# Reordering the matrix engine's work in the opening slot of sequences two to seven

## What is computed

```python
q, k, v = split(x @ Wqkv + bqkv)                       # heads of 32 columns
q_prime = exp(q @ omega - 0.5 * |q|^2); k_prime = exp(k @ omega - 0.5 * |k|^2)
k_sum = sum over rows of k_prime;  k_v = k_prime.T @ v # one per sequence and head
out = (q_prime @ k_v) / (q_prime @ k_sum + 1e-6)
x = layernorm(x + out @ Wout + bout)
x = layernorm(x + x @ weight.T + pooled(x) @ disha)
```

## Time and profile before

| | |
|---|---|
| median of three runs | 2395.49 us (2395.23 to 2403.92) |
| the profiled execution | 2395.51 us, of which its span is 2393.7 us |
| granted TensorE clock, mean | 0.998 of 2.4 GHz |
| PE busy | 2343.8 us, 98% of the span |
| DVE busy | 1956.4 us, 82% |
| ACT busy | 1268.2 us, 53% |
| POOL busy | 286.7 us, 12% |
| SyncE's transfers, issue to landing (median) | 2.1 to 5.0 us |

### The profile page before, as it was taken

The page is one execution under the profiler, slowest core; times in us unless marked ns, Lnnn a source line. Parts: engine busy times, 40 slices in busy tenths (PEclk is TensorE's granted clock), DMA queues, the critical chain, the costliest instruction groups (busy, mean ns, idle before and its releaser), DMA issues.

```text
span 2393.7 us, 55214 instructions
## 1 busy us (share of the span) xinstructions
PE 2343.8 (98%) x21224; PEld 1325.2 (55%) x21224; DVE 1956.4 (82%) x3751; ACT 1268.2 (53%) x2281; POOL 286.7 (12%) x390
## 2 busy tenths in 40 slices
PE   8999999999999999999999999999999999999997
PEld 4545555555555555555555555555555555555554
DVE  6778887888888888887888878888778888788776
ACT  4555555555555555555555555555555555555443
POOL 0001111011111011111011110111110111100221
PEclk9999999999999999999999999999999999999999
DMA  6322332323323323323323233233233232232231
GB/s 209 90 74 71 108 80 82 94 82 94 101 71 99 94 68 108 87 76 96 89 85 104 73 92 95 76 100 98 66 106 90 72 108 76 86 77 59 73 102 50
DMA packets 160277, 213.11 MB, mean 89 GB/s; under 512 B 19376, under 2 KB 119824, under 8 KB 156048
## 3 DMA queue, kind: packets, MB, share of 16 engines
q1 hardware_dynamic: 159440, 208.53, 31.3%
q10 hardware_dynamic: 576, 1.05, 0.1%
HBM read 73.19 MB, written 33.55 MB: 45 GB/s over the span
## 4 chain that ended last, share of the span: by engine, by line
PE 87%; DVE 7%; issue 3%; ACT 2%; SPq 0%; DMA 0%; DVEq 0%; POOL 0%; POOLq 0%; ACTq 0%
PE bank_y L459 24%; PE bank_a L459 24%; PE bank_x L459 12%; PE bank_kf L524 4%; PE bank_qf L578 4%; PE kv_ps L550 3%; PE bank_nm L609 3%; PE bank_x L626 3%; PE bank_nm L626 1%; DVE q_feat_lo L843 1%; PE bank_nm L614 1%; PE kv_ps L556 1%; PE bank_x L486 1%; PE bank_a L486 1%; PE kv_ps L459 1%
## 5 line engine op out<-in xcount | busy, mean ns | idle before, releaser
L706 ACT ACTIVATE q_feat<-bank_qf 128x512 f32<-128x512 f32 x512 | 305.8, 597 | 183.9 <-PE bank_qf L578 183.7
L836 DVE TENSOR_TENSOR k_feat_lo<-k_feat 128x512 bf16<-128x512 f32 x512 | 367.2, 722 | 43.3 <-ACT k_feat L696 43.3
L696 ACT ACTIVATE k_feat<-bank_kf 128x512 f32<-128x512 f32 x512 | 306.0, 598 | 169.7 <-PE bank_kf L524 137.5
L843 DVE TENSOR_TENSOR q_feat_lo<-q_feat 128x1024 bf16<-128x1024 f32 x256 | 313.3, 1224 | 12.3 <-ACT q_feat L706 10.7
L987 POOL TENSOR_TENSOR rstd<-mean_var,minus_half 128x1 f32<-128x1 f32 x128 | 70.3, 549 | 1648.1 <-DVE mean_var L919 1648.1
L976 POOL TENSOR_TENSOR rows<-rows,bias_out 128x512 f32<-128x512 f32 x128 | 168.2, 1325 | 442.1 <-DMA rows<-x 440.2
L524 PE MATMUL bank_kf<-omega_s,stack_k 98*128 98x128 f16 x1920 | 185.8, 219 | 3.1 <-ACT k_feat L696 2.7
L550 PE MATMUL kv_ps<-v_both,k_feat 128*128 128x65 f16 (+1 forms) x2048 | 181.3, 190 | 5.9 <-DVE k_feat_lo L836 5.3
L578 PE MATMUL bank_qf<-stack_q,omega_s 98*128 98x256 f16 x960 | 183.7, 272 | 1.2 <-ACT q_feat L706 1.2
L556 PE MATMUL kv_ps<-v_both,k_feat_lo 128*128 128x33 f16 x2048 | 182.6, 179 | 0.0
L524 PEld LDWEIGHTS bank_kf<-omega_s,stack_k 98*128 98x128 f16 x1920 | 136.1, 97 | 77.6 <-issue 23.5
(11 more groups left out here) (206 smaller groups left out, 5147.7 us busy)
## 6 DMA issues: line engine op xcount, KB each, us to landing
rows<-x SPq DMA_DIRECT2D x128, 256.0 KB, 2.9
out<-rows SPq DMA_DIRECT2D x128, 256.0 KB, 2.1
xt_f<-xt SPq DMA_DIRECT2D x31, 1024.0 KB, 5.0
stack_k<-t_hi_k SPq DMA_DIRECT2D x240, 128.0 KB, 2.4
stack_q<-t_hi_q SPq DMA_DIRECT2D x240, 128.0 KB, 2.4
stack_k<-t_lo_k SPq DMA_DIRECT2D x120, 128.0 KB, 2.4
stack_q<-t_lo_q SPq DMA_DIRECT2D x120, 128.0 KB, 2.4
stack_q<-t_hi_k SPq DMA_DIRECT2D x16, 128.0 KB, 2.5
```

The source lines that it names most:

```text
L696: nc.scalar.activation(k_feat[:, i % 2, :], bank_kf[:, :], ACT.Exp, scale=1.0 / WS).then_inc(S["k_exp"], 1)
L706: nc.scalar.activation(q_feat[:, 2 * pair:2 * pair + 2, :], bank_qf[:, :].rearrange("p (e n) -> p e n", e=2), ACT.Exp, scale=1.0 / WS).the ...
L836: v.tensor_tensor(k_feat_lo[:, u, :], k_feat[:, u, :], k_feat_hi[:, u, :], ALU.subtract).then_inc(S["kfl"], 1)
L843: v.tensor_tensor(q_feat_lo[:, at, :], q_feat[:, at, :], q_feat_hi[:, at, :], ALU.subtract).then_inc(S["qfl"], 2)
```

## The change

A ninth order, `ORDER_NEXT`, is used in the opening slots of b = 2 to 7, six slots in all. It differs from `ORDER` in one line and a half, and no piece is added or removed. TensorE does the second half of FF3' before NM1 and not after it. KF0 moves ahead of the second half of VP1. AT0 and NM2 move behind that half. KF1 and KV0 move ahead of WO0's first half, and NM3 and QF8 between its halves. The orders of ScalarE, VectorE and GpSimd are derived from the same string and change with it. SyncE's order is the same as before.

```diff
@@ -68,6 +68,14 @@
+ORDER_NEXT = """
...
 (the lines ahead of these are those of ORDER; of ORDER:)
-QP2 FF3'. NM1 FF3' VP1. AT0 NM2 Z3' KF0 VP1 QF8 NM3 WO0. KF1 QF9 WO0 KV0 KF2 VP2. AT1 KV1 QF10 VP2 QF11
 (in ORDER_NEXT:)
+QP2 FF3'. FF3' NM1 VP1. KF0 Z3' VP1 AT0 NM2 KF1 KV0 WO0. NM3 QF8 WO0 QF9 KF2 VP2. AT1 KV1 QF10 VP2 QF11
...
@@ -134,7 +142,7 @@
-PE_ORDERS = [pieces(text) for text in (ORDER_FIRST, ORDER, ORDER_LAST, ORDER_K, ORDER_Q, ORDER_0, ORDER_END, "")]
+PE_ORDERS = [pieces(text) for text in (ORDER_FIRST, ORDER, ORDER_LAST, ORDER_K, ORDER_Q, ORDER_0, ORDER_END, "", ORDER_NEXT)]
@@ -297,7 +305,7 @@
-            return 1
+            return 8 if c == 0 and b > 1 else 1
```

More of the change, by code:

```diff
@@ L67 @@
 QP2 FF3'. NM1 FF3' VP1. AT0 NM2 Z3' KF0 VP1 QF8 NM3 WO0. KF1 QF9 WO0 KV0 KF2 VP2. AT1 KV1 QF10 VP2 QF11
+KF3 WO1. QF12 YT0 KV2 KF4 QF13 WO1 QF14 QP3. QF15 XS QP3 KV3 XL0 VP3. VP3 KV4 NM4 XL1 FF0. KF5 YT1 XL2 FF0 XL3 NM5 KV5 KF6
+"""
+ORDER_NEXT = """
+KP0. KF7' Z0' KP0 QN' KF8' KV6' FF1'. KV7' FF1' AT2' KF9' KV8' KP1. NM6' Z1' KP1 KF10' NM7' WO2'. KV9'
+WO2' QF0 KF11' KP2. KV10' AT3' KP2 KF12' KV11' QP0. QF1 QP0 WO3'. KV12' QF2 KF13' WO3' YT2' KP3. KF14'
+QF3 KP3 KV13' QF4 KF15' QP1. KV14' QF5 KN QF6 QP1 FF2'. QF7 KV15' FF2' YT3' KFIN0' VP0. KFIN1' VP0 QP2. Z2' NM0
+QP2 FF3'. FF3' NM1 VP1. KF0 Z3' VP1 AT0 NM2 KF1 KV0 WO0. NM3 QF8 WO0 QF9 KF2 VP2. AT1 KV1 QF10 VP2 QF11
 KF3 WO1. QF12 YT0 KV2 KF4 QF13 WO1 QF14 QP3. QF15 XS QP3 KV3 XL0 VP3. VP3 KV4 NM4 XL1 FF0. KF5 YT1 XL2 FF0 XL3 NM5 KV5 KF6
@@ L152 @@
     "ST0' ST1' LX1 LX0 ST2' ST3' LX3 LX2 STQ NRQ", "XT STK NRK WL", "ST0' ST1' LX1 LX0 ST2' ST3' LX3 LX2",
-    "ST0' ST1' ST2' ST3'"]]
[1 row of a table added]
 A_KINDS = ("KP", "VP", "KN", "KF", "KV", "KFIN", "XS", "XL", "XT", "STK", "NRK", "WL", "WV", "WQ", "WX", "WF", "WE", "WM")
```

## The result

The changed kernel takes 2403.39 us (median of 12 runs, 2399.72 to 2407.13), the kernel before in the same sets 2398.04 us (12 runs, 2395.23 to 2403.92). The ratio is 1.0021, with an interval of 1.0014 to 1.0028: about 5 us slower, small but clear of noise. The forecast was 2396.3 us with a range up to 2401.0, so the time lies outside it. Of the 7.1 us between forecast and time, 2.5 lie in the base: the forecast was put on a median of 2395.49 us from three runs, and twelve runs gave 2398.04. The change was forecast at +0.8 us and came out at +5.3, by the medians.

A forecast was written before the change was run, and what follows sets the result against it. TensorE was taken to bound everything, so only its waits could be won. Four slots at +0.24 us and two at about -0.1 gave +0.8 us on 2395.49: 2396.3 us, range 2391.5 to 2401.

The forecast's parts named there:

- NM1's wait: TensorE's NM1, now behind FF3's second half, never waits: minus 0.10 us in four slots, 1.17 and 1.05 in two.
- KF0's earlier place: KF0 on TensorE moves from 769.80 to 768.73; its stacked keys have 6.2 us to land, so it costs nothing.
- `attn` ahead of the addition: VectorE starts NM1's `attn` 0.13 us before GpSimd's bias addition (769.49 against 769.62), so the addition is held instead.
- The first rival: The addition starts before `attn`, AT0 waits 0.97 us at b = 3; +4.3 us in all, 2399.8 us, chance 0.25.
- KF0's low part under the addition: On VectorE it is held by GpSimd's addition; KV0 starts 0.36 us late in four slots, about 0.6 in two.
- NM4: Late-slot TensorE wait for `q_feat_lo`, which earlier additions might hold; taken as 0, ends -1.3 and +3 us.
- the sum of +0.8: Six opening slots together: four at +0.24 us (+0.96), b = 2 and 7 at about -0.1 each.
- The rival of the backlog: Two additions in a row hold QF9's low part, NM4 waits 1.2 us more per slot; 11.5 us, 2407, chance 0.03.
- The sign "over 75 us": The prediction called itself wrong altogether if the opening slots came out over 75 us, or if another slot moved.
- The bound on gains: Opening slots are 4.9 us longer together than the six slots behind them, taken as the most that could be won.

The follow-up runs named there:

- The narrow late additions: Changed kernel with GpSimd's third and fourth bias additions of each opening slot done on 8 of 512 columns; 2395.5 us, ratio 0.999.
- gates: GpSimd's bias additions wait for certain VectorE instructions in all slots with keys; new order 2382.22 us (0.9937), old order 2381.98 us (0.9936).
- the gates in the opening slots: New order with each bias addition in the six opening slots started only behind a certain VectorE instruction; 2391.65 us, ratio 0.9969.

## Why the prediction was wrong

- **NM1's wait: right.** It never waits after; 2.64 us gained, forecast 2.6. KF0's earlier place costs nothing, as said.
- **`attn` ahead of the addition: right.** The margin was 0.09 us (771.07 to 771.16) where I had 0.13. `attn` keeps its length in all six slots. The first rival, the addition ahead of `attn`, did not happen, though the time it gave, 2399.8, lies nearer to the result than mine.
- **KF0's low part under the addition: right, the split by slots was not.** Forecast 1.76 us, measured 1.77. KV0 lost 2.94 us over six slots where the steps had 2.6, and AT0 0.88 where they had 0.76. That the sums are so near is in part luck. AT0 was to wait at b = 2 and 7 alone, and waited at b = 2, 3 and 4 (0.28, 0.41, 0.19 us). KV0 was to lose 0.36 us in four slots, and lost 0.59 in four. Behind it stands KFIN: a first addition met it in five slots of six (all but b = 5), and I had taken two, as in the profile of before.
- **NM4: this step failed.** The prediction put it at 0, with ends of -1.3 and +3. It became +4.2 us. With KV2's 0.6 that is 4.8 of the 6.3 us by which the six slots exceed the sum of +0.8; the rest is 0.4 at KV0 and AT0 and steps of 0.1 to 0.2 us elsewhere. I had written that the late additions come 1.2 us earlier and may hold QF9's low part where before they held KF2's, so that VectorE is through with KF2 at nearly the same time. QF9's low part was held indeed, but the rest did not come true. The third addition started 20.8 to 22.0 us after QF7's start, against 20.8 to 24.3 before. Z3' and the store were indeed 0.5 to 1.9 us earlier, but the load of the third tile took 3.4 to 4.5 us instead of about 2.9. And the two additions held two instructions and not one. The new order puts QF9's low part behind WO0's addition and statistics on VectorE, where the third addition runs. It slipped in between the two, the fourth addition waited for it, and that pushed the addition onto KF2's low part. The replay took b = 3 alone; at b = 2 the trace of before already showed two held instructions. With 1.1 us already lost at KF0, VectorE had nothing to give back before NM4. The narrow late additions (441.3 us, NM4's loss gone) and QF9's low part moved ahead (444.4 us, NM4's loss 1.9 us) show it from two sides.
- **The rival of the backlog** named this place and this mechanism, but with the first rival added to it (2407 us) and a chance of 0.03. The two were not tied, and it should have had a chance of its own.
- **The sign "over 75 us"** came at b = 2 and 3 (75.08 and 75.46 us), so the prediction was wrong altogether by its own words.
- **The bound on gains** of 4.9 us was too tight, since I had measured the opening slots against neighbours that wait themselves. It did not matter for this change, but it hid what there was to win, by gates and not by an order: 17 us over all slots.

In the profiles the change costs 7.2 us and over the runs 5. If before loses more than 2.6 us at NM1 in a usual execution, that would be the difference, since the new order covers that wait. This is argued, as said above.

## What to carry to other kernels

Where GpSimd and VectorE both work on SBUF, list for each GpSimd instruction which VectorE instructions can stand under it, and let GpSimd wait for a semaphore that VectorE sets just ahead of a stretch with PSUM inputs. In this kernel that brought 0.6% (ratio 0.9937 and 0.9936) with no work left out, and reordering TensorE brought nothing beside it. An order tuned against one profile can rest on a meeting that the next execution doesn't have; look at how often the rare long instruction occurs before you move work to cover it.

## What I had not expected of the hardware

- Two additions ready one behind the other cost VectorE two holds where an instruction slipped in between (b = 3 after): 1.07 us on `q_feat_lo` and 1.07 on the next `k_feat_lo` (2.29 and 1.75 us). In the kernel before they cost one of 0.86 us at b = 3, and two (0.32 and 1.07 us) at b = 2.
- Which VectorE instructions were held does not depend on how long they are. Over the whole trace of before, those with an input in PSUM (L799, L830, L881, L897, L906) were never held. Of those without one, `k_feat_lo`, `q_feat_lo`, `attn`, the last step of KFIN, the cast (128x264) and `den` (128x8) were held. The reciprocal (128x8) and the statistics of `rows` (L788, 128x512), which read SBUF alone too, were not, in any of the 14 and 19 that began under an addition. The Trainium skill says that an instruction with at most one SBUF input does not contend, outside the modes that use both ports ("SBUF — State Buffer", section "Who interferes with whom"). The traces agree for the additions with a PSUM input (of 46 `nm_f` that began under an addition the longest took 0.43 us, as usual) and for the statistics. The cast and `den` have one SBUF input and were held; in which mode they ran no trace shows.
- The load of the third tile took 3.4 to 4.5 us in the six opening slots of the changed kernel, against 2.7 to 3.2 before. Why was not tried. That it is issued earlier is not enough: with the gates in the opening slots, the new order issued this load just as early in five slots of six, and in four of these it took 2.7 to 2.9 us.
